# Handing tokens over from attention to mixture in groups, and a new order of the first three expert tiles

## The reference, cut to what matters

```
x = x + _L0_xattn_ref(_layernorm(x), ctx, ctx)
x = x + _L0_ffn_ref(_layernorm(x), w1, w2)              # ternary feed-forward
x = x + _L1_xattn_ref(_layernorm(x), ctx, ctx)
x = x + _L1_ffn_ref(_layernorm(x), ...)                 # mixture, 8 experts of 176, top 2, shared 352
x = x + _L2_xattn_ref(_layernorm(x), ctx, ctx, gamma)
x = x + _L2_ffn_ref(_layernorm(x), ...)                 # mixture, 32 experts of 128, top 8, shared 256
x = x + _L3_xattn_ref(_layernorm(x), ctx, mask, ...)    # quantized attention
x = x + _L3_ffn_ref(_layernorm(x), ...)                 # mixture, 16 experts of 176, top 4, shared 704
```

## Time and profile before

| | us |
|---|---|
| median of 3 runs | 1243.25 (1241.91 to 1244.57) |
| span of the profiled execution, first to last instruction | 1241.4 |
| PE busy in it | 1074.9 (87%) |
| DVE busy | 919.1 (74%) |
| ACT busy | 783.0 (63%) |
| POOL busy | 543.5 (44%) |

### The profile page before, as it was taken

One profiled execution on the slowest core, in us unless ns is written; L12 is line 12 of the kernel. 1 busy time (PEld: TensorE's weight loads), 2 busy tenths in 40 slices (PEclk: granted clock), 3 DMA queues, 4 the chain that ended last, 5 costly groups with the idle time before them and its releaser, 6 DMA issues. The chain is left out here.

```text
span 1241.4 us, 20766 instructions
## 1 busy us (share of the span) xinstructions
PE 1074.9 (87%) x6773; PEld 771.5 (62%) x6773; DVE 919.1 (74%) x1736; ACT 783.0 (63%) x1232; POOL 543.5 (44%) x672
## 2 busy tenths in 40 slices
PE   4798955799689978999679999999867688999998
PEld 2455523444578855554568888888533476888886
DVE  7677887612678877886788788778777877878876
ACT  4577776499347745776346777777473445677774
POOL 6244456001276613123266666666101027666662
PEclk9798978799789998998789999999978879999999
DMA  5762120476224316431224345333000013443332
GB/s 183 217 200 90 46 76 13 125 190 165 69 85 124 111 35 171 140 116 39 70 79 128 124 135 174 118 125 119 23 9 1 1 44 110 124 124 121 120 118 72
DMA packets 74927, 128.36 MB, mean 103 GB/s; under 512 B 10476, under 2 KB 43948, under 8 KB 74215
## 3 DMA queue, kind: packets, MB, share of 16 engines
q1 hardware_dynamic: 73126, 121.01, 32.7%
q0 software_dynamic: 864, 6.03, 1.4%
q10 hardware_dynamic: 864, 0.39, 0.1%
HBM read 111.36 MB, written 15.45 MB: 102 GB/s over the span
## 5 line engine op out<-in xcount | busy, mean ns | idle before, releaser
L1763 POOL TENSOR_TENSOR f_up_lo<-f_w_up,f_up_hi 128x1024 fp32r<-128x1024 f32 (+1 forms) x76 | 172.9, 2275 | 185.4 <-ACT f_up_hi L1633 165.3
L939 ACT ACTIVATE a_probs<-a_p_sc 128x1024 f32<-128x1024 f32 x192 | 188.6, 1019 | 22.3 <-PE a_p_sc L833 16.0
L1083 DVE TENSOR_REDUCE a_maxes<-a_p_max 128x2 f32<-128x512 f32 x256 | 159.9, 682 | 44.9 <-PE a_p_max L800 44.6
L833 PE MATMUL a_p_sc<-a_q,a_k 75*128 75x256 bf16 (+1 forms) x768 | 117.2, 281 | 11.2 <-ACT a_probs L939 6.8
L1510 PE MATMUL f_p_y<-f_hid_hi,f_down_hi 128*128 128x512 f32 x304 | 120.4, 396 | 2.0 <-DVE f_hid_lo L1869 2.0
L1510 PE MATMUL f_p_y<-f_hid_hi,f_down_lo 128*128 128x512 f32 x304 | 119.7, 394 | 0.0
L1510 PE MATMUL f_p_y<-f_hid_lo,f_down_hi 128*128 128x512 f32 x304 | 119.6, 393 | 0.0
L1500 PE MATMUL f_p_g<-f_x_hi,f_up_hi 128*128 128x512 f32 x268 | 105.9, 395 | 12.6 <-DVE f_x_lo L1978 12.3
L854 PE MATMUL a_p_out<-a_probs,all_v 128*32 128x256 f32 x1536 | 113.6, 412 | 1.6 <-ACT a_probs L939 1.2
L1834 DVE TENSOR_TENSOR f_p_u<-f_p_u,f_x_t 128x512 f32<-128x512 f32 x67 | 46.9, 700 | 85.3 <-PE f_p_u L1500 85.3
L1500 PE MATMUL f_p_g<-f_x_lo,f_up_hi 128*128 128x512 f32 x268 | 105.0, 392 | 0.0
(11 more groups left out here) (361 smaller groups left out, 2500.4 us busy)
## 6 DMA issues: line engine op xcount, KB each, us to landing
f_coef<-coef SPq DMA_DIRECT2D x49, 512.0 KB, 3.6
f_w_up<-in_w SPq DMA_DIRECT2D x76, 256.0 KB, 2.9
a_q<-q_parts SPq DMA_DIRECT2D x48, 288.0 KB
f_w_down<-in_w SPq DMA_DIRECT2D x76, 128.0 KB, 2.0
a_k<-k_plain SPq DMA_DIRECT2D x96, 96.0 KB
a_k<-k_unit SPq DMA_DIRECT2D x24, 192.0 KB
outs<-a_out SPq DMA_DIRECT2D x32, 128.0 KB, 2.0
a_whole<-outs SPq DMA_DIRECT2D x32, 128.0 KB, 2.6
```

The source lines that it names most:

```text
L833: last = nc.tensor.matmul(p_sc[pair % 2][:, h % 2, t * D:(t + 1) * D], k_of(b, h, K_ROWS)[:, t * P:(t + 1) * P], q_of(b, h, K_ROWS), start ...
L939: nc.scalar.activation(probs[b % 2][:, 2 * pair:2 * pair + 2, :, :].rearrange("p h t d -> p h (t d)"), p_sc[pair % 2][:], ACT.Exp, scale=s ...
L1083: nc.vector.tensor_reduce(maxes[b % 3][:, :, h], p_max[:, n % 3, :].rearrange("p (t d) -> p t d", t=NK), axis=AX.X, op=ALU.max, negate=Tru ...
L1763: nc.gpsimd.tensor_tensor(up_lo[slot(t, 2)][:, 0:width], w_up[slot(t, 2)][:, 0:width], up_hi[slot(t, 2)][:, 0:width], ALU.subtract).then_i ...
```

## The change

1. **A `Front` for each mixture**, allocated ahead of its attention and kept across both: `x_t`, the high and low parts of x, the statistics, the router, and the first two weight tiles with their high and low parts (placed over `unit_part`). The tokens are handled in groups: tiles 0-1, 2-3, 4-5, 6, 7 in mixtures 1 and 2, and four pairs in mixture 3. The root is taken by POOL (power of -0.5 and one refinement, five small instructions a group) instead of ACT.
2. **In attention 1 and 2** SP loads the router and the first two weight tiles at b = 10; DVE normalizes groups 0 to 2, makes the operands of groups 0 and 1 and splits the two weight tiles; PE transposes and computes logits between its steps (`turn_front`). Tiles 6 and 7 are added in the mixture, 6 by POOL (`add_seventh`), 7 by DVE. `load_whole` comes one sequence earlier in attention 1, and from b = 13 in attention 2.
3. **Attention 0 and 2** use `PLAIN_ORDER` for b = 14 and 15, where no maxima are left, and ACT takes the third exponential before `copy_out` there.
4. **In all three mixtures** PE's order is now: the three tiles for the first half of the tokens, then for the second half, then the transposition of the coefficients, then the second half of the first down product, then tile 3. Products are numbered by `job(t, c)` = t + 3c. Shared tiles in mixtures 1 and 2 are no longer multiplied by ones.
5. **In mixture 3** the whole normalization still stands at the start of the mixture, now in four groups; logits wait for all four copies, since they go into the bank of the last one. The first two weight tiles are loaded and split in the attention before.
6. The operands of the last attention are placed over `m.v` instead of having tensors of their own.

Core of the diff:

```diff
+def place_last_attention(m):
+    flat = m.v[:].rearrange("p b n -> p (b n)")
...
+class Front:
...
+    def invert_root(self, pool, g):
+        pool.wait_ge(self.var_ready, g + 1)
+        link(tt(y, z, self.half[:, lo:hi], ALU.pow))
+        link(tt(t, y, y, ALU.mult))
+        link(tt(t, t, z, ALU.mult))
+        link(ts(t, t, -0.5, 1.5, ALU.mult, ALU.add))
+        tt(y, y, t, ALU.mult).then_inc(self.root_ready, 1)
...
+                def wholes_at(b):
+                    if layer == 1:
+                        return [b - 2] if b >= 2 else []
+                    if layer == 0 or b < 13:
+                        return [b - 3] if b >= 3 else []
+                    return [b - 3, b - 2] if b == 13 else [b - 2]
...
+                def turn_front(b):
+                    turns, reads = {1: ((9, 12), (10, 13)), 2: ((14, 15), (15, None))}[layer]
...
+                def order_of(b):
+                    if b == 0 and with_max:
+                        return FIRST_ORDER
+                    return STEP_ORDER if with_max and b < LAST_MAX else PLAIN_ORDER
...
 # attention, DVE, layer 2
+                        o.invert(nc, dve, 4, 0, D)
+                        parts.ready(dve, 2, len(CUTS) - 1)
+                        normalize(0)
+                        for t in range(2):
+                            front.split_high(dve, copy, t)
+                        normalize(1)
+                        operands(0)
+                        o.invert(nc, dve, 5, 0, D)
+                        operands(1)
+                        front.keep_logits(dve, 0, p_max[:, 0, :])
+                        normalize(2)
...
 # mixture, PE, layers 1 and 2 (layer 3 alike, with logits first)
+                    gate_up(0, 0)
+                    front.turn(pe, 2, turn_bank[2])
+                    gate_up(1, 0)
+                    gate_up(2, 0)
+                    front.turn(pe, 3, turn_bank[3])
+                    pe.wait_ge(front.x_t_ready, 3)
+                    front.turn(pe, 4, turn_bank[4])
+                    first_down(0)
+                    pe.wait_ge(front.x_t_ready, 4)
+                    for g in range(EARLY_LOGITS[layer], 5):
+                        front.logits(pe, g, turn_bank[3])
+                    gate_up(0, 1)
                     gate_up(1, 1)
-                first_down()
-                gate_up(2, 0)
-                gate_up(2, 1)
+                    gate_up(2, 1)
+                turn_coefficients()
+                first_down(1)
                 pe.wait_ge(x_sum_lo_ready, 4)
...
 # mixture, ACT, layers 1 and 2
+                    silu(0, 0)
+                    split_up(2, UP)
+                    front.copy(act, act_copy, 2, turn_bank[2])
+                    front.high(act, act_copy, 2)
+                    early_high(0, 0)
+                    silu(1, 0)
+                    early_high(1, 0)
+                    silu(2, 0)
+                    for g in (3, 4):
+                        front.copy(act, act_copy, g, turn_bank[g])
+                        front.high(act, act_copy, g)
+                    split_down(1)
+                    score()
```

More of the change, by code:

```diff
@@ L533, with attention @@
 AHEAD = 16
+LAST_MAX = B - AHEAD // HEADS
 SLOTS = 8
-def attention(nc, m, a, layer):
+def attention(nc, m, a, layer, front, o):
     with_max = layer != 1
@@ L778, in _ @@
                         o.store_out(sp, m, b - 1)
-                    if b >= 3:
-                        o.load_whole(sp, m, b - 3)
+                    for b2 in wholes_at(b):
+                        o.load_whole(sp, m, b2)
+                    if layer != 0 and b == 10:
+                        front.load(sp, a)
                     if with_max and b >= 1 and b + 7 < B:
@@ L896, in _ @@
                                          start=True, stop=True).then_inc(m.ternary.meaned, 1)
-                    for what in (PLAIN_ORDER if layer == 1 else STEP_ORDER if b else FIRST_ORDER):
+                    for what in order_of(b):
                         if what == "m":
@@ L1309, in rank_top, with mixture @@
     link(last)
-def mixture(nc, m, a, layer):
+def mixture(nc, m, a, layer, front, o):
     mx = MIXTURES[layer]
@@ L1742, in _ @@
                 split_up(3)
-                silu(2, 0)
+                split_down(2)
                 tile(FIRST)
@@ L2728, in quantized_attention, with _ @@
             with nc.Block() as block:
+                @block.sync
+                def _(sp):
+                    front.load(sp, a)
                 @block.gpsimd
@@ L2732, in _ @@
                         nc.gpsimd.tensor_tensor(m.x[:, i, :], m.x[:, i, :], bias[1][:], ALU.add)
+                    for t in range(2):
+                        front.split_low(pool, t)
                 @block.tensor
@@ L2806, in _ @@
                         copy_p(i)
+                        if i in (3, 4):
+                            front.split_high(act, lambda out, src: nc.scalar.activation(out, src, ACT.Copy), i - 3)
                 @block.vector
@@ L2940, in program @@
             kind, layer = stage
-            if stage == ("ffn", 2):
-                lt = Stage(nc, late, "late")
-                m.raw = [lt.sb(f"raw{n}", [P, NK, D]) for n in range(2)]
-                m.cond = lt.sb("cond", [P, NK, T])
-                m.wk = lt.sb("wk", [P, NK, D])
-                m.wv = lt.sb("wv", [P, NK, D])
-            if kind == "xattn" and layer < 3:
-                attention(nc, m, a, layer)
+            if kind == "xattn" and layer > 0:
+                ahead = ExitStack()
+                st = Stage(nc, ahead, f"p{layer}")
+                front = Front(st, m, layer)
+                o = Outputs(st) if layer < 3 else None
+            if stage == ("ffn", 2):
+                place_last_attention(m)
+            if stage == ("xattn", 0):
+                attention(nc, m, a, layer, None, m.outputs)
+            elif kind == "xattn" and layer < 3:
+                attention(nc, m, a, layer, front, o)
             elif kind == "xattn":
-                quantized_attention(nc, m, a)
-                late.close()
+                quantized_attention(nc, m, a, front)
             elif layer == 0:
@@ L2955, in program @@
             else:
-                mixture(nc, m, a, layer)
+                mixture(nc, m, a, layer, front, o)
+                ahead.close()
             if kind == "ffn" and layer < 3:
```

637 lines of the change are left out of this document (446 added, 191 removed).

## The result

The changed kernel takes 1280.0 us in the median of four runs (1276.8 to 1286.2) against 1242.6 for the kernel before in the same session (1241.9 to 1244.6): ratio 1.0296, 95% interval 1.0267 to 1.0325. That is 3% slower, where 1246.7 was forecast, with a range that ended at 1252. The profiled execution has a span of 1278.8 us against 1241.4, so 37.4 us are to be found. I cut both spans at marks that exist in both, each time the start of an instruction: first and last exponential of an attention, tile 3 of a mixture, the first product of the next stage. The last column is what the prediction has for the stretch.

A forecast was written before the change was run, and what follows sets the result against it. PE is busy 87% of the span, but the change can move only when tile 3 starts in each mixture. −1.0 − 9.1 − 0.8 + 0.3 + 14.0 = +3.4 on the median of 1243.25 gives 1246.7 us, range 1237 to 1252.

The forecast's parts named there:

- the first term of mixture 1: Before mixture 1's opening: the inserted transpositions and logits cost PE some 0.8 us; the mixture opens at 314.5.
- A second term: Attention 1: loading whole results one sequence sooner; the prediction gives it no cost.
- Rival D: Insertions slow the attentions: PE loses about 1.4 us instead of 0.2 in each of four groups; +9 in all; chance 12%.
- if attention 1 or 2 has grown by over 2 us: One of the signs the prediction named in advance as showing it wrong, to be read in the new profile.
- Mixture 1: Tile 3 starts at 352.7 instead of 361.83: −9.1, between −12 and −6; −9.9 from attention 1's last exponential.
- C: In each mixture, the end of DVE's two copies of the transposed coefficients, ahead of the sums of x tile 3 needs.
- Attention 2 and mixture 2: Mixture 2 opens at 599.2 instead of 601.04; tile 3 at 642.0 against 642.86: −0.8, between −5 and +3.
- Mixture 3: Tile 3 at 1051.9 against 1038.80, +13.1, plus 0.9 for PE's half clock: +14.0, between +6.8 and +17.
- The sequence behind C: Mixture 3: tile 2's coefficients issued at C + 5.0, landing at C + 8.8, then POOL's work; tile 3 at C + 13.8.
- POOL's order: Mixture 3: tile 2's multiplications ahead of tile 3's low part make it C + 13.8, not C + 7.5; worth 6.3 us.
- the front: Mixture 3's start: POOL's roots by pairs (+2.1) and logits ahead put the first product at 1013.9 instead of 1010.77, +3.1.
- Attention 0: PLAIN_ORDER in the last two steps brings the last whole results back sooner: −1.0, between −2 and 0.

The follow-up runs named there:

- e1: Changed kernel with only attention 1's router load issued at b = 5 instead of b = 10; 1274.7 us, ratio 1.0242.
- e2: Changed kernel with attention 1 loading each whole result three sequences behind instead of two; 1283.2 us, ratio 1.0288.
- e5: Changed kernel, attention 1: transpositions at b = 11 and 15, first logits at 13, second group's in the mixture, tile 5 inverted before its operands; 1265.4 us.
- e3: Changed kernel, mixture 3: POOL makes tile 3's low part ahead of tile 2's two multiplications; 1271.1 us, ratio 1.0198.
- g4: The e6 kernel with 8 filler matmuls behind each of the first three transpositions in mixture 3; 1274.7 us, ratio 1.0261.
- g1: g2 plus, in mixture 3, e3, e6, coefficients turned before the second half, filler matmuls, and POOL's weight splits after DVE's last normalization; 1246.4 us, ratio 1.0014.
- e7: Changed kernel with a gap of 320 to 448 bytes ahead of the sums of x in every mixture; 1276.7 us, ratio 1.0250.
- g2: Changed kernel with attention 1's transpositions at b = 11 and 14, logits at 13, weight splits behind normalize(1), and e7's gap; 1256.6 us, ratio 1.0098.
- e6: Changed kernel, mixture 3: router logits in their own bank, group by group; DVE copies each group once transposed; 1278.3 us, ratio 1.0262.
- g3: g1 with ACT rounding tile 3's weights ahead of the sums of x in all three mixtures; 1243.3 us, ratio 0.9996.

## Why the prediction was wrong

**The step that failed** is the first term of mixture 1: "The inserted transpositions and logits cost PE some 0.8 us". Where they stood they cost some 18: a wait of 13.0 and the sequence behind it at half clock. I had priced their own durations (0.60 us for four transpositions, 1.85 for the logits), but not whether their inputs are there at b = 9 and 10. PE takes its instructions in order, and ACT's exponentials need the score products that stand behind them. e1 split the wait into router (4.3 us) and tokens (8.7), e2 showed that the other setting of the loads does not close the hole, and e5 gave back 17.2 by the place alone. A second term was put at nothing: the loads of whole results one sequence sooner. They cost 4.4 at sequences 7 and 8, as e2 shows, where PE waits for keys that come behind them on SP. Rival D had the first mechanism, with 1.4 us for each group, 5 to 6 in all, and a condition ("over a microsecond late in a step"); attention 1 alone lost about four times that. The sign was set in the prediction too: I am wrong "if attention 1 or 2 has grown by over 2 us". DVE's waits for whole results, up to 23 us in this attention before, cost nothing because nobody waited for DVE. The change made somebody wait, and it is then the age of the data that counts, not DVE's idle share.

**Mixture 1** was right apart from that: −10.8 for −9.9. C came 30.3 us behind the opening of the mixture (forecast 30.7) and tile 3 7.2 behind C (7.5). **Attention 2 and mixture 2** were −1.5 for −0.8, and the shift between them (−4.8, +3.3) lies as forecast: attention 2 ends by ACT, and DVE's queue keeps the mixture from opening. Two sizes offset each other there: the mixture opens 3.4 us sooner behind the attention's first exponential instead of 1.8, and C follows 36.4 behind the opening instead of 35.3.

**Mixture 3** was right in mechanism, 17.7 for 14.0. The sequence behind C came out within 0.4 us, and e3 confirms the decisive step, POOL's order, with 6.2 us for 6.3. Of the 14.0, 0.9 was PE's start at half clock and lies behind the mark, so at the mark itself 13.1 stood. Mis-sized was the front, 7.0 for 3.1. Of the missing 3.9 us, 2.7 are the logits at half clock (7.01 against 4.34); g4 shows that the clock was down because PE fell idle between the transpositions. POOL's weight splits beside DVE's last normalization are a further 1.3 (2.06 us for a pair against 0.73 in g1, where the splits wait).

**Attention 0** was right at its end, where the change is: from the output copy at b = 13 to the first product behind it 22.2 us before and 20.8 after, −1.5 for −1.0. The +2.3 of the table comes from b = 3, where PE waited 5.0 us for ACT's small transfer of maxima while two loads of 1024 KB were under way; they landed in 11.5 and 11.1 us, before in 6.9 and 8.0, and in 7.1 to 12.7 in the other runs, whose code is the same there. Over those fifteen runs the whole stretch spreads by 7.7 us, and 165.1 before lies inside. That it is chance is argued from this, not shown.

**The 1%** behind tile 3, 4.8 us in three stretches, had no term at all: I took it that PE works as before from there. e7 shows that it is the operands' place in memory. The +1.2 of the ternary layer and the +1.3 of attention 3 are not settled. The first stretch took 71.5 to 73.7 us in the other runs (72.1 before), whose code is the same there; the second was longer than before by 3.7 in g1 and g2 and by −0.6 to +1.6 in the others.

So of 34 us of error 21.6 are attention 1, 4.8 the operands' place, 3.7 mixture 3, 3.3 attention 0, and 2.2 what is not settled; mixtures 1 and 2 gave 1.6 back.

A few of the prediction's sums don't close, none by enough to matter: its parts give 1036.0 for 1036.15, 618.1 for 618.4, and 6.1 of the 6.6 up to the first gate, and PE's second half in mixture 1 was started at 332.8 although its operands were complete only at 333.4.

## What to carry to other kernels

Before an instruction is put into the queue of an engine that feeds others, write down when each of its inputs is ready, through every DMA and round trip, and compare that with the time of its place; its own duration says nothing of its cost. An engine that idles is no proof that its results are early. After a change of buffers look also at the mean duration of the matmuls that weren't changed.

## What the runs showed of the hardware

A matmul of 512 columns in float32 passes took 389 ns in the mean in mixture 2 where all operands began at multiples of 512 bytes in a partition, and for many forms 391 to 398 where some operands lay 128 bytes off and others did not (64 in mixture 3, 192 in mixture 1, alike). A gap of 320 to 448 bytes took the means back to those of the kernel before. Which pair of operands must agree was not tried.

The granted clock was 0.50 in the logits of mixture 3 where PE had been idle for 0.8 to 1.7 us ahead of each transposition (e6), and 1.00 where eight small matmuls stood in three of these pauses and the longest left was 1.08 us (g4).

A DVE sum with two inputs in SBUF took 0.69 us beside an idle POOL, in the changed kernel, and 2.72 beside a subtraction of 2.51 on POOL, in g3. The forecast had leaned on the Trainium skill for this, "SBUF — State Buffer", section "Who interferes with whom": two inputs in SBUF and a GpSimd instruction that reads it lock each other out. The runs agree, both ways: four low parts took 2.49 us where POOL was idle, and 4.63 in the earlier trace rows.
